# Windowed attention and a displaced blur over 32 images: loop jumps marked, a read-back cut in three, two copies and two groups of small matmuls moved

## What is computed

```
x = x + attention(group_norm(x))      # 12 heads of 16 channels, windows of 7 x 7 pixels
x = x + blur(group_norm(x))           # each of 8 channel groups is displaced and blurred 5 x 5

dots = einsum('wnid,wnjd->wnij', q, k) * 16 ** -0.5 + bias[rel_index]
out  = einsum('wnij,wnjd->wnid', softmax(dots), v)      # then w_proj and b_proj
```

## Time and profile before

| what | us |
|---|---|
| median of 3 runs | 6614.67 (6597.92 to 6614.69) |
| profiled execution, its time | 6615.9 |
| its span, first to last instruction | 6614.1 |
| PE busy | 5638.0 (85%), in 97860 matmuls and as many weight loads |
| DVE / ACT / POOL busy | 4323.0 / 3831.3 / 3947.8 |
| granted PE clock, mean | 0.881 |
| packets of the dynamic DMA queue | 1369992, 773.90 MB |

### The profile page before, as it was taken

The page is one execution under the profiler, slowest core; times in us unless marked ns, Lnnn a source line. Parts: engine busy times, 40 slices in busy tenths (PEclk is TensorE's granted clock), DMA queues, the critical chain, the costliest instruction groups (busy, mean ns, idle before and its releaser), DMA issues. The chain is left out here.

```text
span 6614.1 us, 256680 instructions
## 1 busy us (share of the span) xinstructions
PE 5638.0 (85%) x97860; PEld 4650.4 (70%) x97860; DVE 4323.0 (65%) x9677; ACT 3831.3 (58%) x8451; POOL 3947.8 (60%) x4452
## 2 busy tenths in 40 slices
PE   5888888888888888888888888888888888888886
PEld 4777767776777777677767677767777676777775
DVE  4666666766666666667666666666676666666664
ACT  2655555655556565556555565655565556666553
POOL 1466556665556665556665566655566555666565
PEclk9888888988889898889888888888898888998887
DMA  3555665555665556665555655566655556556554
GB/s 80 110 123 122 125 129 121 114 124 121 127 127 116 122 125 126 128 124 111 126 122 119 129 114 119 123 124 128 126 113 125 118 125 131 123 113 126 123 114 76
DMA packets 1371371, 792.20 MB, mean 120 GB/s; under 512 B 1184840, under 2 KB 1234312, under 8 KB 1365768
## 3 DMA queue, kind: packets, MB, share of 16 engines
q1 hardware_dynamic: 1369992, 773.90, 56.0%
HBM read 156.97 MB, written 154.14 MB: 47 GB/s over the span
## 5 line engine op out<-in xcount | busy, mean ns | idle before, releaser
L1188 POOL TENSOR_TENSOR o<-osb,o 128x192 f16<-128x192 f32 x1024 | 590.9, 577 | 1784.1 <-ACT o L830 1755.5
L1182 POOL TENSOR_TENSOR probl<-prob,probh 98x588 f16<-98x588 f32 x1024 | 1340.5, 1309 | 396.7 <-DVE probh L1029 297.9
L628 PE MATMUL pO<-vv,probh 98*49 98x34 f16 x24576 | 1020.8, 225 | 268.4 <-issue 247.7
L628 PEld LDWEIGHTS pO<-vv,probh 98*49 98x49 f16 x24576 | 870.9, 123 | 462.8 <-issue 418.8
L613 PE MATMUL pT<-qst,kst 96*98 96x49 f16 x12288 | 1045.4, 205 | 30.4 <-issue 30.3
L608 PE MATMUL pT<-mov,biasT 128*98 128x98 f16 x6144 | 1014.3, 233 | 51.3 <-ACT om L838 38.2
L613 PEld LDWEIGHTS pT<-qst,kst 96*98 96x98 f16 x12288 | 981.3, 136 | 69.9 <-issue 33.3
L628 PE MATMUL pO<-vv,probl 98*49 98x34 f16 x12288 | 989.7, 228 | 0.0
L608 PEld LDWEIGHTS pT<-mov,biasT 128*98 128x98 f16 x6144 | 842.4, 137 | 147.1 <-issue 71.7
L822 ACT ACTIVATE mov<-pT 12x98 f16<-12x98 f32 x1024 | 247.2, 241 | 1199.5 <-PE pT L597 1196.6
L1014 DVE TENSOR_REDUCE mx<-pS 128x12 f32<-128x588 f32 x1024 | 779.3, 761 | 155.2 <-issue 137.1
(11 more groups left out here) (184 smaller groups left out, 16621.1 us busy)
## 6 DMA issues: line engine op xcount, KB each, us to landing
kst<-kh SPq DMA_DIRECT2D x1536, 98.0 KB, 2.2
qst<-qh SPq DMA_DIRECT2D x1536, 49.0 KB, 2.3
qst<-mix SPq DMA_DIRECT2D x768, 98.0 KB, 2.8
kst<-mix SPq DMA_DIRECT2D x768, 98.0 KB, 2.6
vv<-cv SPq DMA_DIRECT2D x1024, 73.5 KB
out<-xr SPq DMA_DIRECT2D x256, 294.0 KB
xr<-x_scratch SPq DMA_DIRECT2D x64, 882.0 KB
x_scratch<-xm SPq DMA_DIRECT2D x128, 392.0 KB, 3.9
```

The source lines that it names most:

```text
L628: mm = pe.matmul(pO[64 * win:64 * win + NT, OW * hp:OW * hp + OW], b[0:98, p % 2, PW * hp + NT * win:PW * hp + NT * win + NT], vv[:, g % 2 ...
L1182: pool.tensor_tensor(probl[0:98, p % 2, :], prob[0:98, p % 2, :], probh[0:98, p % 2, :], ALU.subtract).then_inc(S["pl_p"], 1)
L1188: pool.tensor_tensor(o16[:, p % 2, C:2 * C], osb[:, p % 2, :], o16[:, p % 2, 0:C], ALU.subtract).then_inc(S["ol_p"], 1)
```

## The change

Five things are done, and all engines' loops are touched:

1. The loop is written with a flag that puts one hint instruction at the top of the body on every engine, naming the branch that jumps back.
2. `read_x1` of the first 42 pixel rows becomes three reads of 14 rows, at p = 1, 2 and 3 (`xr_in` counts two more pairs of transfers); the wait for `y_out` moves from the tail store at p = 31 to the first read at p = 1.
3. `spread_v` is issued ahead of `stack` where both fall on one step.
4. `group_sum` of the next image goes to pQ, at the end of steps 12 and 13; `center` stays at p = 13, `add_eps` moves to p = 14, the power on POOL to p = 15.
5. In `shifted` the six bias matmuls come first, then the twelve score matmuls.

```diff
-                with eng.Fori(1, images - 1) as i:
+                with nc.Fori(1, images - 1, engines=bass.OrderedEngineSet([eng.engine]), hint_back_edge=True) as i:
...
-                if k == EARLY // 2 - 1 and due("y_out", i, 0):
-                    sp.wait_ge(S["y_out"], nth("y_out", i, 0))
...
+                    v = before(v_step, p, prev, att, nxt) if p % PPR == 2 else None
+                    if v:
+                        spread_v(i + v[0], v[1] // 2)
                     qk = before(qk_step, p, prev, att, nxt)
                     if qk and qk[2] % 2:
                         stack(i + qk[0], qk[1], qk[2] // 2)
-                    v = before(v_step, p, prev, att, nxt) if p % PPR == 2 else None
-                    if v:
-                        spread_v(i + v[0], v[1] // 2)
...
-                    if p == 1 and prev:
-                        sp.wait_ge(S["x1_out"], nth("x1_out", i - 1, EARLY * 16))
-                        read_x1(0, EARLY * WS)
+                    if 1 <= p < 4 and prev:
+                        if p == 1:
+                            sp.wait_ge(S["x1_out"], nth("x1_out", i - 1, EARLY * 16))
+                            if due("y_out", i - 1, 0):
+                                sp.wait_ge(S["y_out"], nth("y_out", i - 1, 0))
+                        read_x1(2 * WS * (p - 1), 2 * WS * p)
...
                     pe.matmul(pT[0:98, bank, at:at + PW], biasT[:, PW * hp:PW * hp + PW], mov[:, :],
                               start=(hp % 3 == 0), stop=False, skip_group_check=True)
+                for hp in range(NHP):
+                    bank, at = hp // 3, PW * (hp % 3)
...
-                    if nxt and p in (12, 14):
-                        if att:
-                            pe.wait_ge(S["max_d"], nth("max_d", i, p + 1))
-                        pe.wait_ge(S["gn1_dve"], nth("gn1_dve", i + 1, 2 if p == 12 else 6))
-                        group_sum(1, pS[:, 0, 384:386], gmv[0][:, :, 0] if p == 12 else gv[0]).then_inc(S["gn1_pe"], 1)
-                    if nxt and p in (13, 15):
-                        pe.wait_ge(S["gn1_dve"], nth("gn1_dve", i + 1, 3 if p == 13 else 7))
...
+                    if nxt and p == 14:
+                        pe.wait_ge(S["gn1_dve"], nth("gn1_dve", i + 1, 7))
                     q = qk_step(p, att, nxt)
...
+                    if nxt and p in (12, 13):
+                        if p == 12 and due("qk_dve", i, 12):
+                            pe.wait_ge(S["qk_dve"], nth("qk_dve", i, 12))
+                        pe.wait_ge(S["gn1_dve"], nth("gn1_dve", i + 1, 2 if p == 12 else 6))
+                        group_sum(1, pQ, gmv[0][:, :, 0] if p == 12 else gv[0]).then_inc(S["gn1_pe"], 1)
```

More of the change, by code:

```diff
@@ L231, in build @@
             "c1_pe", "z_act", "z_dve", "c2_pe", "y_dve")}
-        PER = {"x_in": 64, "x1_out": 128, "xr_in": 64, "y_out": 8 * 16, "stack_q": 192 * NCH,
+        PER = {"x_in": 64, "x1_out": 128, "xr_in": 128, "y_out": 8 * 16, "stack_q": 192 * NCH,
                "stack_k": 192 * NCH, "stack_t": 192 * NCH, "gn1_bn": 12, "gn2_bn": 12, "gn1_dve": 8, "gn1_pe": 2, "gn1_pool": 2,
@@ L1081, in body @@
                     if nxt and p == 13:
-                        center(0, i + 1, pS[:, 0, 384:386])
-                    if nxt and p == 15:
-                        add_eps(0, i + 1, pS[:, 0, 384:386])
+                        center(0, i + 1, pQ)
+                    if nxt and p == 14:
+                        add_eps(0, i + 1, pQ)
                         dve.tensor_scalar(gneg[:, :], gmean[0][:, :], -1.0, None, ALU.mult).then_inc(S["gn1_dve"], 1)
@@ L1197, in body @@
                         prob_lo(i + n, q)
-                    if nxt and p == 16:
+                    if nxt and p == 15:
                         pool.wait_ge(S["gn1_dve"], nth("gn1_dve", i + 1, 8))
@@ L1217, in body @@
                         if b == 0:
-                            pool.wait_ge(S["xr_in"], nth("xr_in", i - 1, 64))
+                            pool.wait_ge(S["xr_in"], nth("xr_in", i - 1, 128))
                             pool.wait_ge(S["gn2_dve"], nth("gn2_dve", i - 1, 13))
```

## The result

The changed kernel takes 6774.01 us (median of 4 runs, 6767.95 to 6791.86) where the kernel before takes 6614.68 us beside it: ratio 1.0252, 95% interval 1.0226 to 1.0277. It is 2.5% slower; the forecast was 2.8% faster, and the time lies outside the range. The profiled execution spans 6769.2 us.

What follows compares the result with a forecast made beforehand. Two chains, PE with its stops and SP's queue, were taken to bound the stretch from the jump to p = 7. 171 + 3 - 6 + 15 = 183 us off 6615.9 us gave about 6430 us, range 6260 to 6570 us.

Steps and rivals of the forecast that it cites:

- What bounds the kernel: From the jump to p = 7, PE with its stops and SP's queue run side by side, ending within 0.85 us.
- Part 2, the price of a third: SP's reads at p = 1 to 3: each third takes 4.9 us of data; upper bound 5.7 us of queue hold.
- Part 2, the load of xm: SP's queue ahead of the mix stack: the load goes among the last two thirds, left in the 3.6 us of landing.
- Part 2, the sum: SP's chain to p = 7: mix stack landed at 3156.7, 5.9 us earlier; 171 us for 29 iterations, 3 us for two images.
- Part 1, the hint: At the jump back: removes up to 4.5 us of idle each time, 29 x 4.5 us = 130 us; bounds 0 and 5.2 us.
- Part 2, vv: SP's vv copies issued by 3127.3, 22.9 us earlier, so attend at p = 6 no longer waits its 5.14 us.
- Part 3: vv ahead of the kh stack elsewhere: room at p = 10 and 18, just fits at p = 26; 6 us charged.
- Part 4: Group sums moved from the front of p = 12: net -0.5 us an image, -15 us over 31 images.
- Part 5: Grouping of the matmuls in shifted: put at 0, with at most 0.18 us less for each shifted.
- (c): Rival, 0.06: last two thirds hold the mix stack, deciding from about 95 GB/s downwards; about 6710 us, or 6640 us.
- (a): Rival, 0.22: the read doesn't hold the mix issues, nothing is given back at p = 7; 6230 us, up to 6330 us.
- (b): Rival, 0.17: the hint does nothing and only SP's chain moves; 6533 us.

Runs made afterwards that it cites:

- every-third-row pieces: Changed kernel, its three reads at p = 1, 2 and 3 taking every third row instead of 14 adjacent rows: 6619.17 us, ratio 0.9996.
- with one read: Changed kernel with its first read whole again, 42 rows at p = 1, all else as changed: 6543.18 us, ratio 0.9874.

## Why the prediction was wrong

**What bounds the kernel** was read rightly: two chains from the jump to p = 7, and SP's ends the step. All that PE won at p = 31 and p = 6 (2.6 and 4.5 us, table of steps) went into p = 6 to 7 with 11.5 us.

**Part 2, the price of a third, is the step that failed.** I took 14.6 / 3 = 4.9 us from the 42-row read, "the same rows of data at the same place in the image", though the same 14-row shape stood in the earlier trace rows at 85 GB/s. The changed kernel's packets take 0.586 x 6769.2 - 0.560 x 6614.1 = 263 us more (56.0% before, below), 2.7 us for each of 96 pieces, so 4.9 + 2.7 = 7.6 us for one. By the starts of its packets a piece took 7.7 us in the mean (second table of the experiments). The every-third-row pieces take that back (55.3% of 6622.4 us, 5.4 us each by their starts). My upper bound for a third, 5.7 us, was the queue's hold, not the data.

```profile
q1 hardware_dynamic: 1369992, 773.90, 56.0%
```

**Part 2, the load of xm** was left in the 3.6 us of landing. From the end of the kh stack to the last mix issue I had 9.8 + 7.8 = 17.6 us. The changed kernel took 51.5 - 27.9 = 23.6 us, and even with every third row 47.0 - 26.3 = 20.7 us. The load at p = 2, by the changed kernel's transfer issues (count, KB each, median us to landing; 6.8 us before):

```profile
xm<-in_x SPq DMA_DIRECT2D x32, 1176.0 KB, 12.4
```

With every third row the middle nine tenths of its packets start within 3.6 us (mean over 30 images), mostly between those of the second and the third piece, and 3.1 us are what this kernel still misses of the forecast. That the load is the cause is argued, since no run took it out. One thing speaks against its doing so by itself: with one read it stands ahead of the mix stack too, and there the stack ends 44.5 - 35.1 = 9.4 us after the kh stack, 1.6 us more than its 7.8 us of issues.

**Part 2, the sum.** In us from the start of the qh stack the forecast had the vv copies issued by 17.2, the kh stack by 25.3 and the mix stack by 43.0; measured are 19.1, 27.9 and 51.5, and with every third row 17.7, 26.3 and 47.0. The landing took 2.5 us instead of 3.6, and before 3.8, so `scores` began 6.1 us later than before by this clock (54.0 against 47.9); less about 1.8 us of earlier start (the hint's share in the kernel before) that is 4.3 us a period, against the 4.6 us measured. With pieces near their forecast speed (16.3 us for three against 14.6) the change still wins nothing (ratio 0.9996), so the range would have missed that too. The price of a third explains 2.6 of the 5.3% between forecast and result. The remainder is put down, by argument, to the hint, the xm load, about 1 us up to the end of the kh stack, and the sums.

**Part 1, the hint**, was right in kind and too large. DVE's idle at the jump went as forecast (16.1 us in 29 cases, 0.55 us each), ACT's too (128.6 us ahead of `prob` before, no longer listed). PE's branch still takes 2.3 us in the median, up to 4.9, and with SP's queue as the bound the hint brought 1.8 us a jump, not 4.5.

**Part 2, vv**: `attend` at p = 6 lost its 5 us, as forecast, and that alone brought nothing (0.9992), because the mix stack took over.

**Part 3** has no loss to show in the kernel before (0.9992 in one with part 2's order of p = 2). Chunk 0's stack was close, its scores beginning 2.8 us after its last issue instead of 4.8. But in a kernel no longer held at p = 7 this order costs 0.4%. There chunk 2's stack, for which I wrote that the queue has room at p = 10, lands just as PE needs it; how much of the 0.4% that is stays open.

**Part 4**: forecast -15 us, measured none (0.9994). The group sum lost its wait for `gmv`: 70.1 us in 31 cases, 21.7 of them in one, became 21.3 us in one. Waits for `mx` rose from 73.3 to 112.4 us and for `mov` from 4.8 to 45.0: what I had charged at 0.4 us an image took the whole of it. **Part 5** was right at 0; a `shifted` still takes 0.80 us.

**The rivals.** It went by (c), at 0.06: thirds at 7.1 us and the mix stack held. Its time of 6640 to 6710 us counted on the full hint; with 1.8 us a jump in place of 4.7, 84 us are lost again, and it reads 6724 to 6794 us. The rate that it took stood in the earlier trace rows, measured on this shape, so (c) had more for it than the forecast had. The upper of these two times rests on a loss in part 3 that did not come, so that it covers the measured 6774 us is in part luck: the pieces took 7.7 us and not 7.1. Its limit of 95 GB/s was misreckoned, since two transfers of 294 KB in 6.8 us are 88 GB/s. (a) and (b) are out: the stack was held, and the hint does act.

## What to carry to other kernels

Price a transfer by a row of its own shape, partitions included: here cutting a read into pieces of 14 neighbouring rows cost transfer time (23.0 us against 15.6), while cutting it by channel or every third row cost little or none (14.8 and 16.3 us). When an engine's wait and another queue's chain end together, moving one wait brings nothing; take work out of the chain that both wait for, as with the read put behind the stack (0.9607). And an order that is free under one bound has to be tried again under the next: the same exchange made no difference in the kernel before and cost 0.4% when the read had gone.

## What the runs showed of the hardware

- Three reads of 14 adjacent rows into adjacent partitions against three of 14 rows spread over 42, with the same packets and bytes: 23.1 against 15.0 us from first to last packet start, 1.026 against 0.9952 in the kernel's time.
- A hint for the jump back acts on a body of some 6000 PE instructions. DVE's and ACT's idle at the jump, 4.7 and 4.4 us a time in the mean, goes nearly to nothing. PE's branch takes 4.8 to 5.3 us in the median in the kernels without the hint and 2.2 to 3.6 us in those with it.
- A taken branch stands in the trace as 0.06 us on DVE and its idle beside it as "issue", on PE as a branch of microseconds; why the hint helps PE less is open.
